# Another order of the same instructions in a fused GNN, LSTM and batch-norm kernel: planner durations from the trace, and a table of preferences per operation

## The reference, cut to what matters

```python
# first block
h = relu(einsum('ts,bsh->bth', adj, x @ Wg0 + bg0))
h = relu(einsum('ts,bsh->bth', adj, h @ Wg1 + bg1))
for p in range(1, 5):                       # windows of p nodes along the node axis
    nw = T // p
    wins = h[:, :nw * p, :].reshape(B * nw, p, H)
    last = lstm_last(Wih[p-1], Whh[p-1], bih[p-1], bhh[p-1], wins)   # p steps of an LSTM
    h = h.at[:, arange(nw) * p + (p - 1), :].set(last.reshape(B, nw, H))
x = layernorm(x + h)
# second block
agg = einsum('nm,bmd->bnd', A_hat, x)       # A_hat: adj + I, scaled by its degrees
h = relu(batchnorm(agg.reshape(-1, d) @ W1.T + b1, g1, be1))
out = batchnorm(h @ W2.T + b2, g2, be2)
x = layernorm(x + out)
```

## Time and profile before

| | |
|---|---|
| median of 3 runs | 850.24 us (849.88 to 850.81) |
| the profiled execution's own time | 851.29 us |
| its span, first to last instruction | 849.5 us |
| mean granted TensorE clock | 0.987 |
| PE busy | 813.4 us, 96% of the span |
| DVE busy | 704.7 us, 83% |
| ACT busy | 592.9 us, 70% |
| POOL busy | 68.0 us, 8% |
| DMA | 44.94 MB, mean 53 GB/s |

### The profile page before, as it was taken

One profiled execution on the slowest core, in us unless ns is written; L12 is line 12 of the kernel. 1 busy time (PEld: TensorE's weight loads), 2 busy tenths in 40 slices (PEclk: granted clock), 3 DMA queues, 4 the chain that ended last, 5 costly groups with the idle time before them and its releaser, 6 DMA issues.

```text
span 849.5 us, 15294 instructions
## 1 busy us (share of the span) xinstructions
PE 813.4 (96%) x4872; PEld 518.7 (61%) x4872; DVE 704.7 (83%) x1795; ACT 592.9 (70%) x1186; POOL 68.0 (8%) x58
## 2 busy tenths in 40 slices
PE   9999999999999999999999999999999988999984
PEld 7666666666666666666666676666665654333442
DVE  5577979887988788878987898898889887577995
ACT  4577767776777677767776777677777752991488
POOL 0000000000000000000000000000000001000674
PEclk9999999999999999999999999999999989999998
DMA  5100010012001100110011001010010101244245
GB/s 194 46 26 1 21 55 1 27 49 76 2 26 49 74 0 25 49 70 4 25 49 54 20 25 50 26 51 25 26 50 5 47 25 51 87 136 147 76 155 192
DMA packets 17691, 44.94 MB, mean 53 GB/s; under 512 B 2032, under 2 KB 3184, under 8 KB 17520
## 3 DMA queue, kind: packets, MB, share of 16 engines
q1 hardware_dynamic: 17648, 44.39, 14.6%
HBM read 27.61 MB, written 16.78 MB: 52 GB/s over the span
## 4 chain that ended last, share of the span: by engine, by line
PE 75%; DVE 11%; issue 9%; ACT 4%; POOL 0%; ACTq 0%; DVEq 0%; POOLq 0%
PE gate_bank L731 15%; PE gate_bank L732 14%; PE gate_bank L716 8%; PE gate_bank L747 6%; PE gate_bank L757 6%; PE front_bank L643 3%; PE back_bank L689 3%; PE front_bank L654 3%; DVE bn L941 3%; PE front_bank L648 3%; PE front_bank L660 3%; PE gate_bank L740 3%; ACT z L859 2%; PE back_bank L697 1%; PE back_bank L699 1%
## 5 line engine op out<-in xcount | busy, mean ns | idle before, releaser
L731 PE MATMUL gate_bank<-h_hi,w_hi 128*128 128x256 f16 (+2 forms) x528 | 165.4, 313 | 5.9 <-DVE h_lo L1034 4.4
L809 ACT ACTIVATE gate_i<-gate_bank,lstm_bias 128x256 f32<-128x256 f32 (+2 forms) x176 | 100.0, 568 | 98.4 <-PE gate_bank L757 76.6
L732 PE MATMUL gate_bank<-h_hi,w_lo 128*128 128x256 f16 (+2 forms) x528 | 164.8, 312 | 0.0
L809 ACT ACTIVATE gate_o<-gate_bank,lstm_bias 128x512 f32<-128x512 f32 (+2 forms) x176 | 99.6, 569 | 31.7 <-PE gate_bank L757 22.6
L747 PE MATMUL gate_bank<-h_lo,w_hi 128*128 128x256 f16 (+2 forms) x384 | 117.6, 306 | 0.0
L731 PE MATMUL gate_bank<-s_hi,w_hi 128*128 128x256 f16 (+2 forms) x384 | 112.8, 302 | 2.2 <-DVE s_hi L1031 2.1
L732 PE MATMUL gate_bank<-s_hi,w_lo 128*128 128x256 f16 (+2 forms) x384 | 112.6, 302 | 0.0
L1018 DVE SCALAR_TENSOR_TENSOR gate_f<-gate_o,gate_f 128x512 f32<-128x512 f32 (+2 forms) x176 | 93.8, 539 | 20.0 <-ACT gate_f L815 17.8
L809 ACT ACTIVATE gate_g<-gate_bank,lstm_bias 128x256 f32<-128x256 f32 (+2 forms) x176 | 99.6, 566 | 4.4 <-PE gate_bank L740 2.0
L757 PE MATMUL gate_bank<-s_lo,w_hi 128*128 128x256 f16 (+2 forms) x384 | 100.4, 302 | 0.3 <-DVE s_lo L1034 0.3
L815 ACT ACTIVATE gate_f<-cell 128x512 f32<-128x512 f32 (+2 forms) x176 | 88.0, 507 | 9.3 <-DVE cell L1009 3.6
(11 more groups left out here) (162 smaller groups left out, 1571.6 us busy)
## 6 DMA issues: line engine op xcount, KB each, us to landing
x_front<-in_x SPq DMA_DIRECT2D x16, 512.0 KB, 4.1
rows_sb<-in_x SPq DMA_DIRECT2D x16, 512.0 KB, 3.3
x_kept<-normed_sb SPq DMA_DIRECT2D x16, 512.0 KB, 2.7
z<-x_kept SPq DMA_DIRECT2D x16, 512.0 KB, 3.7
out<-z SPq DMA_DIRECT2D x15, 512.0 KB, 3.1
z<-in_wr SPq DMA_DIRECT2D x1, 1536.0 KB, 6.4
out<-z SPq DMA_DIRECT2D x2, 256.0 KB, 2.2
wih_sb<-in_wih SPq DMA_DIRECT2D x1, 192.0 KB, 2.5
```

Source lines behind the costliest of these rows:

```text
L731: mm(dst, w[0], v[0], start=start, stop=False)
L732: mm(dst, w[1], v[0], start=False, stop=False)
L809: ins = activation(acts[gate][h][:, 0:n], gate_bank[h][bank_of(job, gate)][:, 0:n], ACT.Tanh if gate == "g" else ACT.Sigmoid, bias=lstm_bi ...
```

## The change

The reference, the instructions and their tiles stay. What changes is what `plan_order` works with, and so the order of the instructions on PE, ACT, DVE and POOL.

- Matmuls that read `h_hi` and `h_lo` get a longer duration (`seen_us`, at 2.3 columns per ns in place of 2.4), and so does a pair of `mix` matmuls.
- `EARLIER` can hold several needs; `mix0` gets a second one, the last `z` product of five halves before, with 4.0 us from PE to PE.
- `AHEAD_OP` gives 74 operations a lead of their own, by engine, stream and operation, added to those of the three tables. 36 entries are for PE, 19 for ACT and 19 for DVE.

```diff
-MIX_US = 2 * matmul_us(2 * P, 1)
+def seen_us(columns, passes):
+    return passes * (columns / 2.3 + 2.5) / 1e3
+
+
+MIX_US = 2 * matmul_us(2 * P + 7, 1)
...
             for gate in gates:
-                ops.append(("PE", (job, "gate", gate), matmul_us(n, 3), [(prev, "low")]))
+                ops.append(("PE", (job, "gate", gate), seen_us(n, 3), [(prev, "low")]))
         else:
             for gate in "igf":
-                ops.append(("PE", (job, "input", gate), matmul_us(n, 3), [(prev, "act", bank_reader(prev, gate))]))
+                ops.append(("PE", (job, "input", gate), seen_us(n, 3), [(prev, "act", bank_reader(prev, gate))]))
...
-            ops.append(("PE", (job, "input", "o"), matmul_us(n, 3), [(job, "act", "i")]))
+            ops.append(("PE", (job, "input", "o"), seen_us(n, 3), [(job, "act", "i")]))
...
 EARLIER = {
-    ("mix0", "product", 0, 0): (1, ("mix1", "out", 1)),
+    ("mix0", "product", 0, 0): ((1, ("mix1", "out", 1)), (5, ("back", "z", 3))),
...
-SIGNAL_US = {"PE": {"ACT": 0.21, "DVE": 0.2}, "ACT": {"PE": 0.29, "DVE": 0.16},
+SIGNAL_US = {"PE": {"ACT": 0.21, "DVE": 0.2, "PE": 4.0}, "ACT": {"PE": 0.29, "DVE": 0.16},
...
+AHEAD_OP = {
...
+    ('PE', 'front', ('mix1', 'product', 0, 0)): 0.15,
+    ('PE', 'front', ('mix1', 'product', 1, 0)): -0.2,
+    ('PE', 'even', (('lstm', 1, 0), 'gate', 'i')): 0.05,
+    ('ACT', 'even', (('lstm', 1, 0), 'act', 'o')): -1.9,
...
+    ('ACT', 'even', (('lstm', 2, 0), 'tanh')): -0.9,
...
+    ('PE', 'even', (('lstm', 2, 1), 'gate', 'i')): 1.75,
...
+    ('ACT', 'even', (('lstm', 3, 0), 'tanh')): 1.95,
...
+    ('PE', 'even', (('lstm', 4, 1), 'input', 'o')): 1.65,
...
+    ('PE', 'even', (('lstm', 4, 3), 'gate', 'i')): 1.4,
+    ('ACT', 'even', (('lstm', 4, 3), 'act', 'o')): 1.85,
+    ('ACT', 'even', (('lstm', 4, 3), 'tanh')): -1.2,
...
+    ('PE', 'odd', (('lstm', 2, 1), 'input', 'g')): 1.6,
+    ('PE', 'odd', (('lstm', 2, 1), 'input', 'f')): 1.6,
+    ('PE', 'odd', (('lstm', 2, 1), 'high', 'g')): 1.55,
+    ('PE', 'odd', (('lstm', 2, 1), 'gate', 'i')): 1.8,
...
+    ('DVE', 'odd', (('lstm', 4, 2), 'new')): -1.05,
...
+    ('DVE', 'back', ('back', 'stats', 0)): -0.4,
+    ('DVE', 'back', ('back', 'stats', 1)): -0.35,
...
+}
...
-    return (AHEAD.get((engine, stream), 0) + AHEAD_KIND.get((engine, *kind), 0)
+    return (AHEAD_OP.get((engine, stream, op), 0) + AHEAD.get((engine, stream), 0) + AHEAD_KIND.get((engine, *kind), 0)
             + AHEAD_LAST.get((stream, from_last), 0))
...
-                if op in EARLIER and q >= EARLIER[op][0]:
-                    needs.append((q - EARLIER[op][0], EARLIER[op][1]))
+                needs += [(q - by, x) for by, x in EARLIER.get(op, ()) if q >= by]
```

More of the change, by code:

```diff
@@ L190 @@
 EARLIER = {
-    ("mix0", "product", 0, 0): (1, ("mix1", "out", 1)),
[L192 to L197, removed]
+    ("mix0", "product", 0, 0): ((1, ("mix1", "out", 1)), (5, ("back", "z", 3))),
+    ("mix1", "out", 0): ((1, (LSTM_JOBS[0], "gate", "o")),),
+    ("mix1", "out", 1): ((1, (LSTM_JOBS[1], "gate", "o")),),
+    (LSTM_JOBS[0], "gate", "i"): ((2, (LSTM_JOBS[-1], "act", "o")),),
+    (LSTM_JOBS[0], "act", "o"): ((2, (LSTM_JOBS[-1], "hidden")),),
+    (LSTM_JOBS[0], "high"): ((2, ("back", "tokens", 1, 1)),),
+    ("back", "tokens", 0, 0): ((1, ("back", "z_stats", 3)),),
 }
-SIGNAL_US = {"PE": {"ACT": 0.21, "DVE": 0.2}, "ACT": {"PE": 0.29, "DVE": 0.16},
+SIGNAL_US = {"PE": {"ACT": 0.21, "DVE": 0.2, "PE": 4.0}, "ACT": {"PE": 0.29, "DVE": 0.16},
              "DVE": {"PE": 0.18, "DVE": 0.13, "ACT": 0.13, "POOL": 0.16}, "POOL": {"DVE": 0.2}}
@@ L212 @@
 AHEAD_LAST = {("back", 3): 0.15, ("front", 1): 0.1, ("back", 1): -0.2, ("front", 0): -0.05, ("odd", 0): -0.05}
+AHEAD_OP = {
+    ('PE', 'front', ('lin1', 'product', 0, 2)): -0.15,
+    ('PE', 'front', ('lin1', 'product', 1, 0)): -0.2,
+    ('PE', 'front', ('lin1', 'product', 1, 1)): -0.1,
+    ('PE', 'front', ('mix1', 'product', 0, 0)): 0.15,
+    ('PE', 'front', ('mix1', 'product', 1, 0)): -0.2,
+    ('PE', 'even', (('lstm', 1, 0), 'gate', 'i')): 0.05,
+    ('ACT', 'even', (('lstm', 1, 0), 'act', 'o')): -1.9,
+    ('PE', 'even', (('lstm', 1, 1), 'gate', 'o')): 0.15,
+    ('ACT', 'even', (('lstm', 2, 0), 'tanh')): -0.9,
+    ('DVE', 'even', (('lstm', 2, 0), 'high')): -0.3,
+    ('PE', 'even', (('lstm', 2, 1), 'gate', 'i')): 1.75,
+    ('ACT', 'even', (('lstm', 2, 1), 'act', 'g')): -0.35,
+    ('DVE', 'even', (('lstm', 2, 1), 'high')): -0.5,
+    ('DVE', 'even', (('lstm', 2, 1), 'low')): -0.45,
+    ('PE', 'even', (('lstm', 3, 0), 'gate', 'g')): 0.05,
+    ('ACT', 'even', (('lstm', 3, 0), 'tanh')): 1.95,
+    ('PE', 'even', (('lstm', 3, 1), 'input', 'g')): -0.1,
+    ('PE', 'even', (('lstm', 3, 1), 'high', 'g')): -0.4,
+    ('DVE', 'even', (('lstm', 3, 2), 'high')): 0.65,
+    ('PE', 'even', (('lstm', 4, 0), 'gate', 'i')): -0.25,
+    ('DVE', 'even', (('lstm', 4, 0), 'new')): -0.5,
+    ('PE', 'even', (('lstm', 4, 1), 'input', 'o')): 1.65,
+    ('PE', 'even', (('lstm', 4, 1), 'gate', 'o')): 0.6,
+    ('ACT', 'even', (('lstm', 4, 1), 'act', 'i')): -0.85,
+    ('ACT', 'even', (('lstm', 4, 1), 'act', 'o')): 0.95,
+    ('ACT', 'even', (('lstm', 4, 2), 'act', 'o')): -0.6,
+    ('DVE', 'even', (('lstm', 4, 2), 'high')): -0.4,
+    ('PE', 'even', (('lstm', 4, 3), 'high', 'i')): 0.4,
+    ('PE', 'even', (('lstm', 4, 3), 'high', 'g')): 0.75,
+    ('PE', 'even', (('lstm', 4, 3), 'gate', 'i')): 1.4,
+    ('ACT', 'even', (('lstm', 4, 3), 'act', 'o')): 1.85,
+    ('ACT', 'even', (('lstm', 4, 3), 'tanh')): -1.2,
+    ('DVE', 'odd', (('lstm', 1, 0), 'high')): -0.15,
+    ('DVE', 'odd', (('lstm', 1, 0), 'low')): -0.2,
+    ('PE', 'odd', (('lstm', 1, 1), 'gate', 'i')): -0.2,
+    ('ACT', 'odd', (('lstm', 1, 1), 'act', 'i')): 0.4,
+    ('ACT', 'odd', (('lstm', 1, 1), 'tanh')): -0.75,
+    ('DVE', 'odd', (('lstm', 2, 0), 'high')): 0.25,
+    ('PE', 'odd', (('lstm', 2, 1), 'input', 'i')): 0.25,
+    ('PE', 'odd', (('lstm', 2, 1), 'input', 'g')): 1.6,
+    ('PE', 'odd', (('lstm', 2, 1), 'input', 'f')): 1.6,
+    ('PE', 'odd', (('lstm', 2, 1), 'high', 'g')): 1.55,
+    ('PE', 'odd', (('lstm', 2, 1), 'gate', 'i')): 1.8,
+    ('DVE', 'odd', (('lstm', 2, 1), 'cell')): -0.15,
+    ('PE', 'odd', (('lstm', 3, 0), 'gate', 'i')): -0.15,
+    ('PE', 'odd', (('lstm', 3, 0), 'gate', 'o')): -0.25,
+    ('ACT', 'odd', (('lstm', 3, 0), 'act', 'i')): -0.3,
+    ('DVE', 'odd', (('lstm', 3, 0), 'new')): 0.8,
+    ('PE', 'odd', (('lstm', 3, 1), 'input', 'f')): -0.15,
+    ('PE', 'odd', (('lstm', 3, 1), 'high', 'i')): -0.25,
+    ('ACT', 'odd', (('lstm', 3, 1), 'act', 'i')): 0.7,
+    ('ACT', 'odd', (('lstm', 3, 1), 'act', 'f')): -0.05,
+    ('PE', 'odd', (('lstm', 3, 2), 'high', 'i')): 0.4,
+    ('PE', 'odd', (('lstm', 3, 2), 'high', 'g')): 0.7,
+    ('PE', 'odd', (('lstm', 3, 2), 'gate', 'i')): 0.35,
+    ('PE', 'odd', (('lstm', 3, 2), 'gate', 'o')): 0.85,
+    ('ACT', 'odd', (('lstm', 3, 2), 'act', 'i')): -1.1,
+    ('ACT', 'odd', (('lstm', 4, 0), 'act', 'o')): -1.1,
+    ('ACT', 'odd', (('lstm', 4, 1), 'act', 'f')): -0.25,
+    ('PE', 'odd', (('lstm', 4, 2), 'input', 'f')): -0.45,
+    ('PE', 'odd', (('lstm', 4, 2), 'high', 'i')): -0.3,
+    ('PE', 'odd', (('lstm', 4, 2), 'input', 'o')): -0.05,
+    ('DVE', 'odd', (('lstm', 4, 2), 'new')): -1.05,
+    ('PE', 'odd', (('lstm', 4, 3), 'input', 'g')): -0.1,
+    ('DVE', 'back', ('back', 'residual', 0)): -0.25,
+    ('DVE', 'back', ('back', 'stats', 0)): -0.4,
+    ('DVE', 'back', ('back', 'stats', 1)): -0.35,
+    ('DVE', 'back', ('back', 'moments', 0)): 0.15,
+    ('DVE', 'back', ('back', 'moments', 1)): 0.2,
+    ('DVE', 'back', ('back', 'normed', 0)): -0.3,
+    ('PE', 'back', ('back', 'mix', 0, 2)): 0.7,
+    ('ACT', 'back', ('back', 'mixed', 0)): -0.55,
+    ('ACT', 'back', ('back', 'z_stored', 3)): -0.45,
+    ('DVE', 'back', ('back', 'z_stats', 3)): 0.15,
+}
@@ L275, in cut_order @@
             if all(c[k] == c[k0] for c in chunks.values() for k in range(k0, k1))
-            and all(q + 2 * k0 >= EARLIER.get(op, (0,))[0] for c in chunks.values() for q, op in c[k0])]
+            and all(q + 2 * k0 >= by for c in chunks.values() for q, op in c[k0] for by, _ in EARLIER.get(op, ()))]
     return chunks, max(runs, key=lambda r: r[1] - r[0])
```

## The result

The changed kernel takes 839.84 us (median of 4 runs, 839.04 to 840.99), the kernel before 850.06 us beside it. The ratio is 0.9879, 95% interval 0.9862 to 0.9896: 10.2 us or 1.2% less. The forecast was 845.2 us, so the direction was right and the gain twice what I gave it.

The account below looks back on a forecast made before the run. The prediction took PE, 96% busy, as the bound. Rotations 1.8 + drain 3.2 + clock 1.3 - new holes 1.3 = 5.0 us off the 850.24 us median gave 845.2 us, range 839 to 853.

Parts of the forecast that it names:

- PE bounds the kernel, and the order can only win back its holes: Whole kernel: PE busy 96% of the span; only its idle or lower-clock time can move, for 5.0 us in sum.
- The reading of the rotation: Five loop rotations: ready windowed matmuls put ahead of `mix0` remove its wait for `h1T`; at most 3.75 us, 1.8 taken.
- The start: Before 176 us: PE idles 2.1 us in 170, so nothing much to win there.
- The drain: After the last rotation: 8.6 us of PE idle time, 6.4 open to reordering, half taken, 3.2 us.
- the clock: Behind the drain's 3.0 us wait: a 1.2 GHz stretch costs 2.5 us, gone if the wait shortens; 1.3 us taken.
- the signs of being wrong: A rotation longer than 86.0 us, the drain keeping its 3 us wait, or L643 waiting for a DMA.
- New holes: Seven rotations or parts: late-ready operations preferred on PE leave it idle, 0.2 us each, 1.3 us taken off.
- The durations: Planner's PE durations: no cost on the chip by themselves; they decide only whether a planned order meets the chip as planned.
- The 5-halves entry: Need of `mix0` for the `x_front` load: costs nothing, with about 9 us of slack.
- The larger gain: Rival: both chains end together; the 3.0 us wait, low clock and five steady waits vanish; some 10 us, 840; chance 0.12.
- late picks on PE: Slower rival: recurrent products put ahead of ready work leave holes in seven rotations, 858 us; chance of slower 0.21.

Follow-up runs that it names:

- the filled wait: Kernel before with 12 unread matmuls of 512 columns in the drain's 3.0 us wait: 849.62 us, ratio 0.9991.
- the rearranged drain: Changed kernel with the lists of its first three chunks and its last one rearranged, loop chunk untouched: 838.88 us, ratio 0.987.

## Why the prediction was right and wrong, by its steps

**PE bounds the kernel, and the order can only win back its holes.** Right. Matmul counts are the same, and the 11.7 us gained are distances between starts on PE. The direction was right as well; the sum of 5.0 us was less than half of what came. By its terms: rotations 6.0 for 1.8, start 2.9 for nothing, drain and clock 2.8 for 4.5, new holes nothing for -1.3, together 11.7.

**The reading of the rotation** failed, and it is the step that made the forecast half of what came. I wrote that windowed matmuls stood ready behind the wait for `h1T`, that 0.9 us of them ahead of `mix0` would remove it, bounded the term at 3.75 us by the view of waits, and took 1.8. It was 6.0. The half was a guess, with no row behind it; all five waits went, 4.4 us by the starts. Two things were wrong in the reading. The matmuls weren't ready: their chain needs 3.4 us from its last product, and with the move made as I described it the kernel gets 6.5 us slower. It pays only with more ready work ahead of it, as the changed kernel has it. And the bound was too low: of the 7.7 us lost in the rotations the view of waits shows 3.6 and the windows 4.2, since a hole shorter than the overlap of two matmuls is shown by neither, and a longer one is shown too short. The prediction had 0.91 us by the starts for one wait beside the 0.75 of the view, and took the 0.75.

**The start** I left at nothing, on 2.1 us of idle time in 170. By the distances between starts 4.6 us were lost there, and 2.9 of them went. The same misreading, in a smaller place. Which reorderings won them was not examined.

**The drain** I put at 3.2 us and the clock at 1.3, together 4.5; it was 2.8. The long wait stayed, 2.88 for 3.00 us, with the same chain behind it, and in both kernels the halves drain one after the other. That the drain keeps this wait is one of the signs of being wrong that the prediction named. The term of the clock was mis-sized by its own logic too: 2.5 us of slower matmuls are worth 1.2 us where the chain through ACT and DVE goes on meanwhile, as the filled wait showed.

**New holes**, 1.3 us off for leads of up to 1.8 us: none came in the rotations. The experiment with one entry less shows that a sum by entries had no ground.

**The durations** cost nothing by themselves and decide whether the plan is met: the first half is refuted as a statement on this part alone (durations without the table, 866.8 us); on the second half there is only the planner's own reckoning. (The old durations were also further off than the prediction said: 0.1425 for 0.149 us is 4% short on windowed reads, and only `mix` was 2% short.) Replayed with the new durations, the lists end (first `mix0` to last `z`) at 707.1 us for the kernel before and 696.6 for the changed one; the traces have 710.1 and 698.4. With the old durations they end at 695.9 and 686.1. Both rank the two lists alike, by 10.5 and 9.8 us. So it isn't shown that the old durations stood in the way of this order; what they did was to fix which order the table gives. These four are computed, not measured.

**The 5-halves entry**: no effect, as expected. The planner gives the same lists, operation by operation, with it and without it, so it wasn't run. The one wait of `mix0` (L724) for a DMA in the profile, 0.5 us, falls in the first 25 us, where no half lies five back.

**The rivals.** The larger gain gave 840 us and stood at 0.12; the time is right and its mechanism isn't, for neither the 3 us wait nor the low clock vanished. What it had right is that all five steady waits can go at once. Slower orders do exist close by (durations alone, one entry less, old durations), but whether late picks on PE made them slow wasn't examined, and the changed kernel isn't among them.

**Open** is, besides the small holes and the start, why the rearranged drain won only about 1 of its 3.7 us. Nor was it tried whether a table searched on the old durations would find an order as good.

## What to carry to other kernels

Measure the idle time of a saturated TensorE by the distances between starts, not by the idle time beside modelled ends: here 4.2 us of idle time in the rotations were 7.7 us of loss. Ahead of a link of a recurrent chain TensorE needs as much ready work as the chain's trip through the other engines takes (3.2 to 3.5 us at the place tried here); before moving work into a wait, look at when its operand lands, for what stands behind a wait may not be ready either. And a table of leads for a list scheduler is one searched point together with the durations: here each part taken alone, and the table less one entry, was slower than no change at all; judge an entry by a run, not by its size.

## What the runs showed of the hardware that I had not expected

The low clock behind a 3.0 us wait costs less than its slower matmuls: 5.6 us at the 1.2 GHz level (granted clock 0.50) held the chain up by 1.2 us in the profiled execution. Filling the wait with unread matmuls kept the granted clock at 1.00 there.
